# Two NF4 rounds in each output-projection step, and the layer norm's chain at its end, in a decoder layer on one core

## The chip, the core and the metric

The kernel runs on one core of a Trainium2 chip. The metric is the device time of one execution in microseconds (us). Engines: PE is the matrix engine, DVE, ACT and POOL the vector, scalar and GpSimd engines, SP the engine that here only issues DMAs; ACT and POOL issue some as well.

## The reference

One post-norm decoder layer in float32, for a batch of 4 sequences of 512 positions, width 512, 16 heads of 32:

```
x = layernorm(x + self_attention(x, wq, wk, wv, wo))        # 8 kv heads, rotary embedding, causal
x = layernorm(x + cross_attention(x, ctx, Wq, Wkv, Wout))   # causal mask over the first 512 of 1601 keys
x = layernorm(x + ffn(x, nf4(w1), nf4(w2), nf4(w3)))        # silu(x w1') * (x w2'), then w3'; inner width 1408
```

The three FFN weights pass through an NF4 round trip inside the kernel: blocks of 64 are scaled by their largest magnitude, each value goes to the nearest of 16 levels, and it is multiplied by a scaler that was itself quantised to 8 bits.

## The kernel before, in words

**Steps.** Eight blocks b = 0..7 (0 to 3 are self attention of the four sequences, 4 to 7 cross attention) of eight steps p = 0..7; a step (b, p) handles two heads. PE's program is one list written out by hand (from L1100 on): scores of the heads (`scores`, L935, turned: keys on partitions), row maxima two steps ahead (`maxima`, L902), weighting of the values (`weigh`, L959), the products of the next block's q, k, v (`make`, L886 to L888), and in step (b, 1) the output projection of block b - 1 (`project_out(b-1, k)`, k = 0, 1; same lines; 24 products each). Each fp32 product is three products of high and low parts.

**Banks.** All units that PE writes for one use (four score units `exp`, `rows`, `raw`, `out`, `round`) share two PSUM banks in the order of `ring_order()`: unit i waits until unit i - 2 has been read. A `round` is freed by DVE's `scale_rounded` (L1651), an `exp` by ACT's exponential (L1327), an `out` by DVE's two additions of `add_residual` (L1521, L1522). The maxima have one PSUM tile of their own: in self attention DVE's reduction (L1497) of one unit must end before PE's next; in cross attention (L1492) the two heads are waited for one by one.

**NF4 rounds.** 48 rounds, 20 during self attention and 28 during cross. One round takes a chunk of the divided weights: SP loads it (`load_round`: `x4`, L478, then the stores of the round before, L488, then the scalers `dqb`, L482), four comparison passes 0 to 3 run on ACT (`exceed`, L1304) or DVE (L1637), PE sums them (`rounding`, L1061, 16 products), DVE multiplies (L1651). Pass 3 overwrites the loaded chunk and waits for the other three; there is one such buffer, so the load of round u waits for PE's round u - 1. `round_of(b, p)` gives each step at most one round: (1,1) to (3,4), and (4,1) to (7,4). `scalar_passes` gives ACT pass 0, in self attention's steps 3 and 4 passes 0, 1, 3, in its step 5 passes 0, 3. ACT runs pass 0 ahead of the last exponential of the step.

**Stacks.** The heads' q and k go by six SP DMAs (`load_stacks`, L453 to L465) into four slots; SP loads those of step (b, p) + 3 after the round's load in its list. They wait for the last score unit of the step before, which frees the slot, and in self attention for POOL, which rotates and splits q and k (L668 to L685). In self attention only step 5 of a block makes nothing for the next block on PE; POOL rotates there.

**Layer norm** of block b - 1 in steps 1 to 3 of block b, on DVE: step 1 `add_residual` 0, maxima, `moments` 0 (L1528), `add_residual` 1; step 2 `moments` 1 after the first maxima, `spread` (mean, variance and a Newton inverse root on 128x4 values: L1814 to L1834, a chain of 16 tiny dependent instructions and more) after pass 3, ahead of the last maxima and of `scale_rounded`; step 3 `scale_rows` (L1538, four of 128x512). SP stores the result in step 4. POOL's `weighed` (L697 to L701) is started in every even step by DVE's `over_sums` (L1515), which stands just ahead of pass 3.

**FFN.** After block 7, `FTILES` tiles g; PE makes two hidden products (L1171), and from g = 2 on `ffn_contribute(g-1)` (L1201). At g = 1 PE does the last two output projections; the first contribution waits for both `out` units to be read. DVE at g = 1: `add_residual` 0, `moments` 0, `layer_norm` of two rows' tiles, and only then `add_residual` 1; the other half of the norm at g = 2.

Of the kernel before, what the change touches and what calls it, by code (L numbers as in the profile page):

```python
# [30 lines left out]
NP = NH // 2  # L31
# [67 lines left out]
FIRST_ROUND = NP + 1  # L99
CROSS_HOME = B * NP + 1  # L100


def round_of(b, p):

    at = b * NP + p
    u = at - FIRST_ROUND if at < FIRST_ROUND + SELF_ROUNDS else at - CROSS_HOME + SELF_ROUNDS if at >= CROSS_HOME else -1
    return u if 0 <= u < ROUNDS else None
# [8 lines left out]
def scalar_passes(u):  # L116

    b, p = divmod(u + FIRST_ROUND, NP)
    return {3: (0, 1, 3), 4: (0, 1, 3), 5: (0, 3)}.get(p, (0,)) if u < SELF_ROUNDS and b < B - 1 else (0,)
# [23 lines left out]
def ring_order():  # L143
# [3 lines left out]
    for b in range(NB):  # L147
        for p in range(NP):
# [5 lines left out]
            order += [("exp", b, p, 2), ("exp", b, p, 3)]  # L154
            order += [("raw", b + 1, what) for what in made(b + 1, p)]
            if p == 1 and b > 0:
                order += [("out", b - 1, k) for k in range(2)]
# [4 lines left out]
            if round_of(b, p) is not None:  # L162
                order.append(("round", round_of(b, p)))
# [3 lines left out]
def decoder_layer(nc, xs_dram, xt_dram, ctx_dram, w_self, w_cross, rope_dram, w_nat, w_t, nf_steps, nf_limits,  # L167
# [56 lines left out]
    with ctx:  # L224
# [207 lines left out]
        def _(sp):  # L432
# [88 lines left out]
            for b in range(NB):  # L521
                for p in range(NP):
# [6 lines left out]
                    if round_of(b, p) is not None:  # L529
# [8 lines left out]
                    if (b, p) == (1, 0):  # L538
# [10 lines left out]
                    if (b, p) == (NB - 1, 5):  # L549
                        store_round(ROUNDS - 1)  # L550
# [325 lines left out]
        def _(pe):  # L876
# [222 lines left out]
            for b in range(NB):  # L1099
                for p in range(NP):  # L1100
# [25 lines left out]
                    if p == 1 and b > 0:  # L1126
                        project_out(b - 1, 1)
                    if fore and (whats or p == 1):
# [3 lines left out]
                    if round_of(b, p) is not None:  # L1132
                        rounding(round_of(b, p))
# [87 lines left out]
        def _(act):  # L1221
# [134 lines left out]
            for b in range(NB):  # L1356
                for p in range(NP):
                    turn1, u = after(b, p, 1), round_of(b, p)
                    mine = scalar_passes(u) if u is not None else ()
# [14 lines left out]
                    if 0 in mine:  # L1374
# [551 lines left out]
```

## Time and profile before

| | us |
|---|---|
| median of 3 runs | 1232.68 (1232.57 to 1236.12) |
| profiled execution: its own time | 1232.01 |
| its span, first to last instruction | 1230.1 |
| PE busy | 1065.7 (87%) |
| DVE busy | 776.0 (63%) |
| ACT, POOL busy | 471.8, 464.5 (38% each) |
| mean granted PE clock | 0.939 |

The span is what the trace's clock counts; the execution's own time is 1.9 us longer. Of the chain of work that ended last, PE is 60%, DVE 18%, ACT 6%, DMA 6%. PE's clock is granted at 2.4 GHz (1.0) or 1.2 GHz (0.5). Steps 0 to 7 of block 1 run from 165.7 to 288.4 us, block 2 to 413.2, block 3 to 534.4, the cross blocks to 639.9, 755.2, 860.4 and 946.8, and the FFN from there to the end.

### The profile page before, as it was taken

The page shows a single profiled execution, that of the slowest core. Times are in us where ns is not written, and L with a number is a line of the kernel's source. Part 1 is how long each engine was busy: PE and PEld are TensorE (multiplying, and loading weights), DVE is VectorE, ACT ScalarE, POOL GpSimd, SP SyncE. Part 2 cuts the span into 40 slices and gives each one's busy share as a digit, 9 for nine tenths or more (in the row PEclk, how much of TensorE's full clock was granted, in tenths as well). Part 3 has the DMA queues.
Part 4 walks back from the last instruction along what each step waited for, and adds up shares of the span by engine and source line. Part 5 has one row for each costly group of instructions (what it writes and reads, how often), then busy time and mean ns, then how long its engine had stood idle before and what let it go on. Part 6 is the DMA issues. An engine that isn't in the chain of part 4 may idle for free.

```text
span 1230.1 us, 17427 instructions
## 1 busy us (share of the span) xinstructions
PE 1065.7 (87%) x6248; PEld 689.7 (56%) x6248; DVE 776.0 (63%) x1564; ACT 471.8 (38%) x580; POOL 464.5 (38%) x500
## 2 busy tenths in 40 slices
PE   6888888987988887888989778889878899999995
PEld 4545445543554353455556445555634788888884
DVE  6786657666676567547775775677494745455444
ACT  3342352645354543552553464446445021202110
POOL 4537874785378534232242232223435500000000
PEclk9798899999998898998899888989989999999998
DMA  6731563476356734733664483447556210302010
GB/s 205 213 68 43 140 165 107 133 203 179 102 152 159 201 108 118 168 68 93 148 177 95 104 208 87 105 130 175 146 126 180 83 51 1 103 1 69 1 69 34
DMA packets 81809, 145.13 MB, mean 118 GB/s; under 512 B 14984, under 2 KB 31728, under 8 KB 81468
## 3 DMA queue, kind: packets, MB, share of 16 engines
q1 hardware_dynamic: 68812, 104.03, 32.3%
q0 software_dynamic: 11888, 39.73, 11.2%
q8 instruction: 50, 0.82, 0.3%
q10 hardware_dynamic: 1024, 0.26, 0.1%
q14 instruction: 35, 0.29, 0.1%
HBM read 78.09 MB, written 23.73 MB: 83 GB/s over the span
## 4 chain that ended last, share of the span: by engine, by line
PE 60%; DVE 18%; ACT 6%; DMA 6%; issue 5%; POOL 3%; SPq 2%; ACTq 1%; DVEq 0%; POOLq 0%
PE att_pv L959 10%; PE att_scores_T L886 7%; PE att_scores_T L1201 7%; PE att_scores L1171 6%; PE att_pv L1171 6%; PE att_scores_T L887 6%; PE att_scores_T L888 6%; PE att_scores L902 6%; PE att_scores_T L935 3%; ACT att_probs L1327 3%; DMA att_k_stack<-att_k_lo 2%; DVE att_scores L1492 2%; DMA att_nf_home<-nf_dequantised_rows 2%; PE att_scores_T L1061 2%; DVE att_mx L1497 2%
## 5 line engine op out<-in xcount | busy, mean ns | idle before, releaser
L1327 ACT ACTIVATE att_probs<-att_scores_T 128x1024 f32<-128x1024 f32 (+2 forms) x256 | 219.6, 884 | 296.6 <-PE att_scores_T L935 293.9
L959 PE MATMUL att_pv<-att_probs,att_v 128*32 128x512 f32 (+3 forms) x1024 | 221.4, 557 | 1.3 <-POOL att_probs L741 0.9
L959 PE MATMUL att_pv<-att_probs,att_ones 128*32 128x512 f32 (+3 forms) x1024 | 221.4, 557 | 0.0
L1497 DVE TENSOR_REDUCE att_mx<-att_scores 128x2 f32<-128x1024 f32 x124 | 151.7, 1223 | 102.7 <-PE att_scores L902 101.6
L902 PE MATMUL att_scores<-att_k_stack,att_q_stack 96*128 96x256 f32 (+1 forms) x504 | 170.1, 415 | 43.8 <-DVE att_mx L1497 20.8
L935 PE MATMUL att_scores_T<-att_q_stack,att_k_stack 97*128 97x512 f32 (+2 forms) x512 | 147.1, 399 | 31.7 <-DVE att_nf_zone L1651 26.2
L1492 DVE CUSTOM_DVE_ANT_0 att_scores<-att_scores,att_cmask 128x128 f32<-128x128 f32 (+3 forms) x256 | 120.9, 512 | 72.0 <-PE att_scores L902 71.7
L741 POOL TENSOR_SCALAR_AFFINE_SELECT att_probs<-att_probs 128x256 f32<-128x256 f32 x128 | 59.0, 461 | 251.4 <-ACT att_probs L1327 249.0
L902 PEld LDWEIGHTS att_scores<-att_k_stack,att_q_stack 96*128 96x128 f32 x504 | 91.5, 203 | 88.9 <-DVE att_mx L1497 28.2
L935 PEld LDWEIGHTS att_scores_T<-att_q_stack,att_k_stack 97*128 97x128 f32 x512 | 90.9, 202 | 75.6 <-DVE att_nf_zone L1651 39.8
L959 PEld LDWEIGHTS att_pv<-att_probs,att_v 128*32 128x32 f32 x1024 | 51.3, 115 | 112.1 <-issue 91.3
L697 POOL TENSOR_TENSOR att_pv_raw<-att_pv_raw,att_sums_turned 128x512 f32<-128x512 f32 x32 | 45.5, 1423 | 166.7 <-DVE att_sums_turned L1515 166.7
L1407 ACT ACTIVATE att_probs<-att_scores 128x512 f32<-128x512 f32 x44 | 26.3, 598 | 213.7 <-PE att_scores L1171 213.7
L1742 DVE TENSOR_TENSOR att_probs<-att_probs,att_pv 128x512 f32<-128x512 f32 x44 | 30.2, 687 | 114.3 <-PE att_pv L1171 114.3
L886 PE MATMUL att_scores_T<-att_x_hi,att_w_hi 128*128 128x512 f32 x160 | 70.4, 440 | 21.8 <-ACT att_probs L1327 11.7
L887 PE MATMUL att_scores_T<-att_x_lo,att_w_hi 128*128 128x512 f32 x160 | 67.7, 423 | 0.0
L888 PE MATMUL att_scores_T<-att_x_hi,att_w_lo 128*128 128x512 f32 x160 | 67.2, 420 | 0.0
L886 PE MATMUL att_scores_T<-att_w_hi,att_o_hi 128*128 128x512 f32 x128 | 51.8, 404 | 5.7 <-ACT att_probs L1327 5.7
L1521 DVE TENSOR_TENSOR att_y<-att_scores_T,att_y 128x512 f32<-128x512 f32 x16 | 11.1, 691 | 69.9 <-PE att_scores_T L888 69.9
L886 PEld LDWEIGHTS att_scores_T<-att_x_hi,att_w_hi 128*128 128x128 f32 x160 | 33.2, 207 | 35.0 <-ACT att_probs L1327 18.3
L888 PE MATMUL att_scores_T<-att_w_hi,att_o_lo 128*128 128x512 f32 x128 | 51.2, 400 | 0.0
L887 PE MATMUL att_scores_T<-att_w_lo,att_o_hi 128*128 128x512 f32 x128 | 51.1, 400 | 0.0
(251 smaller groups left out, 2181.6 us busy)
## 6 DMA issues: line engine op xcount, KB each, us to landing
att_q_stack<-att_q_hi SPq DMA_DIRECT2D x128, 128.0 KB, 3.1
att_probs<-nf_x SPq DMA_DIRECT2D x28, 352.0 KB, 3.6
att_nf_home<-nf_reciprocals POOLq DMA_DIRECT2D x48, 176.0 KB, 4.2
att_q_stack<-att_q_lo SPq DMA_DIRECT2D x64, 128.0 KB, 3.6
att_k_stack<-att_k_hi SPq DMA_DIRECT2D x64, 128.0 KB, 3.4
att_nf_home<-nf_x SPq DMA_DIRECT2D x20, 352.0 KB, 3.5
w_nf<-att_nf_zone SPq DMA_DIRECT2D x192, 22.0 KB, 2.6
att_k_stack<-att_k_hi SPq DMA_DIRECT2D x64, 64.0 KB, 2.7
```

The source lines that it names most:

```text
L741: pool.affine_select(out=v, in_=v, compare_op=ALU.is_ge, fill=0.0, base=0, pattern=[[0, 2], [1, P]], channel_multiplier=-1).then_inc(kept, 1)
L886: T.matmul(out, a_hi, b_hi, start=start, stop=False)
L887: T.matmul(out, a_hi, b_lo, start=False, stop=False)
L888: return T.matmul(out, a_lo, b_hi, start=False, stop=stop)
L902: last = T.matmul(sco[:, r, 0:width], qst[0:96, s, r, P * t:P * t + P], kst[0:96, r if crossed(b) else 0, s, 0:width], start=True, stop=True)
L935: last = T.matmul(bank[:, at:at + S - q0], kst[0:97, r if crossed(b) else 0, s, P * t:P * t + P], qst[0:97, s, r, q0:S], start=True, stop= ...
L959: last = T.matmul(pv[HD * j:HD * j + HD, sums, q0:S], lhs, pr[:, at:at + S - q0], start=(t == 0), stop=(t == TT - 1))
L1171: last = T.matmul(bank, ffn_weight(w, f, kt), x[:, kt, :], start=kt == 0 and i == 0, stop=kt == KT - 1 and i == 1)
L1201: last = T.matmul(fpy[:, t, :], h[:, g % 2, P * t:P * t + P], ffn_rows(f), start=f == 0 and i == 0, stop=f == FT - 1 and i == 1)
L1327: A.activation(probs_of(b, r)[:, 1024 * h:1024 * h + w], bank[:, 0:w], ACT.Exp, scale=SCALE).then_inc(st_free, 1)
L1492: V.tensor_tensor_reduce(out=sco[:, r, 0:width], in0=sco[:, r, 0:width], in1=cmask[:, S - width:S], scale=1.0, scalar=NEG, op0=ALU.add, op ...
L1497: V.tensor_reduce(mx[:, p % 2, :].rearrange("p (r t) -> p r t", r=2)[:, :, t], sco[:, :, :], AX.X, ALU.max).then_inc(sc_free, 1)
```

## The change

1. Rounds. `round_of` becomes a list `ROUND_STEPS`. Step (b, 1) has two rounds, `mid` and `end`, for b = 1 to 6; self attention's step 5 has none, and (3, 4) has none any more; the last round, the 48th, is the `mid` of (7, 1), where it was in (7, 4). ACT's passes 0, 1, 3 stay in (1,3), (1,4), (2,3), (2,4).
2. Step (b, 1) of PE is: `project_out` 0, maxima 2, round `mid`, `project_out` 1, then `make` (x0, for a cross block to come), maxima 3, `weigh`, round `end`. Before, `make`'s first half stood ahead of the projection, and there was no `mid`.
3. Step (b, 1) of DVE ends with `scale_rounded(end)`, `moments` 1, `spread`, and the cut of x0. `scale_rows` moves to step 2, two tiles after the first maxima and two after the second. SP stores in step 3.
4. SP's list: the stacks come ahead of the round's load, except the stacks of a new block's first step (`fresh`, issued in step 5), which stay behind it.
5. FFN: both `add_residual` and both `moments` at g = 1; `layer_norm` of each half at g = 2 and g = 3.

```diff
+def round_steps():
+    steps = []
+    for b in range(1, NB):
+        for p in range(NP):
+            if b < B and p == 5 or b == B - 1 and p > 3 or (b, p) in ((1, 0), (B, 0)):
+                continue
+            steps += [(b, p)] * (2 if p == 1 else 1)
+    return steps[:ROUNDS]
+def rounds_of(b, p):
+    us = [u for u, step in enumerate(ROUND_STEPS) if step == (b, p)]
+    return tuple((us if p == 1 else [None] + us) + [None, None])[:2]
 def scalar_passes(u):
-    return {3: (0, 1, 3), 4: (0, 1, 3), 5: (0, 3)}.get(p, (0,)) if u < SELF_ROUNDS and b < B - 1 else (0,)
+    return (0, 1, 3) if b < B - 1 and p in (3, 4) else (0,)
...
 # SP
-                    if round_of(b, p) is not None:
-                        load_round(round_of(b, p))
-                    if nxt and pairs(*nxt) >= SLOTS:
+                    fresh = nxt and nxt[0] > b and nxt[1] == 0
+                    if nxt and pairs(*nxt) >= SLOTS and not fresh:
                         load_stacks(*nxt)
...
+                    for u in rounds_of(b, p):
+                        if u is not None:
+                            load_round(u)
+                    if fresh:
+                        load_stacks(*nxt)
...
-                    if p == 4 and b > 0:
+                    if p == 3 and b > 0:
                         store(b - 1)
 # PE
-                    make(b + 1, whats, 0)
                     if p == 1 and b > 0:
                         project_out(b - 1, 0)
-                    if fore and not (crossed(b) and p == 0):
                         maxima(*fore, 2)
-                    make(b + 1, whats, 1)
-                    if p == 1 and b > 0:
+                        if mid is not None:
+                            rounding(mid)
                         project_out(b - 1, 1)
+                        for half in range(2):
+                            make(b + 1, whats, half)
...
 # DVE
+                    if p == 1 and b > 0:
+                        maxima(*fore, 0)
+                        maxima(*fore, 1)
+                        exceeds(mid, range(4))
+                        add_residual(b - 1, 0)
+                        maxima(*fore, 2)
+                        if mid is not None:
+                            scale_rounded(mid)
+                        moments(b - 1, 0)
+                        exceeds(end, (1, 2))
+                        add_residual(b - 1, 1)
+                        exceeds(end, (3,))
+                        maxima(*fore, 3)
+                        if end is not None:
+                            scale_rounded(end)
+                        moments(b - 1, 1)
+                        spread(range(TT))
+                        for what in made(b + 1, p):
+                            cut_raw(b + 1, what)
+                        continue
                     if p == 2 and b > 0:
-                        moments(b - 1, 1)
-                    if p == 3 and b > 0:
                         scale_rows(range(0, 2), TT - 1)
...
                 if g == 1:
-                    add_residual(NB - 1, 0)
-                    moments(NB - 1, 0)
-                    layer_norm(range(2))
-                    add_residual(NB - 1, 1)
-                    moments(NB - 1, 1)
-                if g == 2:
-                    layer_norm(range(2, TT))
+                    for k in range(2):
+                        add_residual(NB - 1, k)
+                    for k in range(2):
+                        moments(NB - 1, k)
+                if g in (2, 3):
+                    layer_norm(range(2 * (g - 2), 2 * (g - 2) + 2))
```

## Rows read from the trace of the kernel before

**Rows 1.** View of waits, whole run: engine, line, released by; total us, times, longest.
```profile
PE att_scores_T L935 <- DVE att_nf_zone L1651: 26.2, 11, 5.6
PE att_scores_T L1061 <- ACT att_nf_home L1304: 6.9, 2, 3.5
PE att_scores_T L1201 <- DVE att_y L1522: 3.9, 1, 3.9
```
**Rows 2.** View of waits, 635 to 870 us.
```profile
PE att_scores L902 <- DMA att_k_stack<-att_k_lo: 8.0, 4, 3.5
```
**Rows 3.** View of waits, 911 to 935 us: steps (7,3) and (7,4).
```profile
PE att_scores_T L1061 <- DVE att_probs L1637: 4.5, 2, 2.7
```
**Rows 4.** Timeline of PE, (1,1) to (1,3): start, us, what, [idle before].
```profile
187.15 0.40 PE L886 MATMUL att_scores_T<-att_w_hi,att_o_hi 128*128 128x512 f32 x1
192.73 0.63 PE L902 MATMUL att_scores<-att_k_stack,att_q_stack 96*128 96x512 f32 x2
195.03 0.63 PE L1061 MATMUL att_scores_T<-att_nf_zone,att_nf_steps 128*32 128x352 bf16 x12
215.38 1.13 PE L935 MATMUL att_scores_T<-att_q_stack,att_k_stack 97*128 97x512 f32 x2 [3.66 <-DVE att_nf_zone L1651]
```
**Rows 5.** Timeline of DVE, step (1,2): first of `spread`, and the maximum behind it.
```profile
207.68 0.06 DVE L1814 MEMSET att_newton<- 128x4 f32 x1
213.67 1.23 DVE L1497 TENSOR_REDUCE att_mx<-att_scores 128x2 f32<-128x1024 f32 x1
```
**Rows 6.** Timeline of POOL, step (4,2), during `spread`.
```profile
574.57 1.51 POOL L697 TENSOR_TENSOR att_pv_raw<-att_pv_raw,att_sums_turned 128x512 f32<-128x512 f32 x1 [1.44 <-DVE att_sums_turned L1515]
```
**Rows 7.** Timeline of DVE in the FFN: the norm's second half, POOL idle.
```profile
979.53 0.06 DVE L1814 MEMSET att_newton<- 128x2 f32 x1
982.16 1.00 DVE L1538 TENSOR_SCALAR att_y<-att_y,att_mean_var,att_newton 128x512 f32<-128x512 f32 x2
```
**Rows 8.** Timeline of DVE, (4,3): cut of an x half; two tiles scaled.
```profile
581.28 1.22 DVE L1443 TENSOR_TENSOR att_x_lo<-att_raw,att_x_hi 128x1024 fp32r<-128x1024 f32 x1
583.25 1.09 DVE L1538 TENSOR_SCALAR att_y<-att_y,att_mean_var,att_newton 128x512 f32<-128x512 f32 x2
```
**Rows 9.** Timeline of PE, steps (4,1) to (4,3).
```profile
565.97 0.34 PE L1061 MATMUL att_scores_T<-att_probs,att_nf_steps 128*32 128x352 bf16 x4
568.79 0.48 PE L902 MATMUL att_scores<-att_k_stack,att_q_stack 96*128 96x256 f32 x2
581.42 0.80 PE L935 MATMUL att_scores_T<-att_q_stack,att_k_stack 97*128 97x512 f32 x1 [2.54 <-DVE att_nf_zone L1651]
```
**Rows 10.** View of groups of instructions, shapes apart: busy us, mean ns, idle before.
```profile
L1528 DVE BATCH_NORM_STATS2 att_stats<-att_y 128x6 f32<-128x512 f32 x32 | 20.5, 681 | 0.2
```
**Rows 11.** Stretches: us; busy PE, PEld, DVE, ACT, POOL; clock; DMA share; GB/s.
```profile
382.80:389.60 6.80, 5.86 (x28) 3.08 (x32) 2.87 (x4) 2.78 (x3) 6.42 (x5) 0.50 0.31 81
580.70:590.90 10.20, 9.05 (x38) 6.63 (x39) 6.21 (x18) 3.62 (x5) 1.43 (x3) 0.50 0.64 153
642.20:645.60 3.40, 3.40 (x24) 2.42 (x17) 1.97 (x10) 1.17 (x2) 0.35 (x1) 0.50 0.86 248
263.30:341.80 78.50, 67.13 (x449) 39.15 (x445) 52.43 (x80) 33.35 (x37) 43.00 (x46) 1.00 0.56 152
```
**Rows 12.** Timeline of SP and PE around the start of step (6,0).
```profile
753.52 0.61 SPq L461 DMA_DIRECT2D att_k_stack<-att_k_lo  x1
757.23 0.51 PE L902 MATMUL att_scores<-att_k_stack,att_q_stack 96*128 96x256 f32 x2 [1.63 <-DMA att_k_stack<-att_k_lo]
```
**Rows 13.** Timeline of SP and PE in step (1,5).
```profile
254.80 0.60 SPq L465 DMA_DIRECT2D att_k_stack<-att_k_lo  x1
258.50 0.63 PE L1061 MATMUL att_scores_T<-att_nf_zone,att_nf_steps 128*32 128x352 bf16 x12 [3.46 <-ACT att_nf_home L1304]
```
**Rows 14.** Tile att_nf_home: a pass on ACT; its DMAs to landing.
```profile
L1304 ACT ACTIVATE att_nf_zone<-att_nf_home,att_nf_limits x24: 1449/1458/1464, 181.8 to 492.5; 128x1408 bf16<-128x1408 bf16 x24
DMA to landing us min/median/max: 1.9/3.6/8.6
```

More of the change, by code:

```diff
@@ L154, in ring_order @@
             order += [("exp", b, p, 2), ("exp", b, p, 3)]
+            mid, end = rounds_of(b, p)
+            if p == 1 and b > 0:
+                order.append(("out", b - 1, 0))
+                if mid is not None:
+                    order.append(("round", mid))
+                order.append(("out", b - 1, 1))
             order += [("raw", b + 1, what) for what in made(b + 1, p)]
-            if p == 1 and b > 0:
-                order += [("out", b - 1, k) for k in range(2)]
             if (b, p) == (0, 2):
@@ L161, in ring_order @@
                 order.append(("dq",))
-            if round_of(b, p) is not None:
-                order.append(("round", round_of(b, p)))
+            if end is not None:
+                order.append(("round", end))
     return order + [("out", NB - 1, k) for k in range(2)]
@@ L1131, in _ @@
                     weigh(b, p, 1)
-                    if round_of(b, p) is not None:
-                        rounding(round_of(b, p))
+                    if end is not None:
+                        rounding(end)
                     if (b, p) == (0, 2):
@@ L1357, in _ @@
                 for p in range(NP):
-                    turn1, u = after(b, p, 1), round_of(b, p)
-                    mine = scalar_passes(u) if u is not None else ()
+                    turn1, (mid, end) = after(b, p, 1), rounds_of(b, p)
+                    mine = scalar_passes(end) if end is not None else ()
                     exponential(b, p, 0)
@@ L1373, in _ @@
                         hi_of_x(*halved(b, p))
-                    if 0 in mine:
-                        exceed(u, 0)
+                    if mid is not None:
+                        for k in scalar_passes(mid):
+                            exceed(mid, k)
+                    elif 0 in mine:
+                        exceed(end, 0)
                     exponential(b, p, 3)
-                    for k in mine[1:]:
-                        exceed(u, k)
+                    for k in mine if mid is not None else mine[1:]:
+                        exceed(end, k)
                     if (b, p) == (B - 1, 0):
@@ L1686, in _ @@
                         largest_behind(b, p, 1)
+                    if p == 2 and b > 0:
+                        scale_rows(range(2, TT), TT - 1)
                     if p % 2 == 0 and pairs(b, p) > 0:
                         sums_of(G)
[L1689 to L1690 removed]
                     if (b, p) == (0, 2):
@@ L1698, in _ @@
                         order_dequantised()
-                    exceeds(u, (1, 2))
-                    if closing:
-                        add_residual(b - 1, 0)
+                    exceeds(end, (1, 2))
                     if fore:
@@ L1704, in _ @@
                         largest_behind(b, p, 2)
-                    if closing:
-                        moments(b - 1, 0)
-                        add_residual(b - 1, 1)
                     if p % 2 == 0 and pairs(b, p) > 0:
@@ L1711, in _ @@
                         reciprocals()
-                    exceeds(u, (3,))
-                    if p == 2 and b > 0:
-                        spread(range(TT))
+                    exceeds(end, (3,))
                     if crossed(b + 1):
@@ L1721, in _ @@
                         largest_behind(b, p, 3)
-                    if u is not None:
-                        scale_rounded(u)
+                    if end is not None:
+                        scale_rounded(end)
                     if fore and not early:
```

27 lines of the change are left out of this document (13 added, 14 removed).

## Prediction

> **What bounds the kernel now.** I read the page first, then the view of waits, then the timelines around its longest waits, then the stretches at low clock. The page has PE busy 87% of the span and 60% of the ending chain, DVE 18%: the kernel is PE's list of work plus the places where PE stands still. The waits say where. 26.2 us in 11 waits are PE's second score unit waiting for DVE's last act of a round; 6.9 us are rounds waiting for a pass on ACT; 3.9 us is the FFN's first contribution waiting for `add_residual` [rows 1]. Four waits for stacks make 8.0 us in the cross blocks [rows 2], and two rounds waiting for DVE's passes 4.5 us in (7,3) and (7,4) [rows 3]. The reader is to see that nearly all of them concern the rounds. The clock is the second half of the story: after a wait PE often runs at 1.2 GHz for a stretch, 3.4 to 10.2 us long, in which it is busy nearly all the time [rows 11]; a matmul-bound stretch at half clock costs about half its length.
>
> **Part 1, the norm's chain.** The 3.66 us ahead of 215.38 is one of the seven entries to a step (b, 3) behind the 26.2 us [rows 4]: `spread` stands ahead of the last maxima and the round's multiplication and takes 213.67 - 207.68 = 6.0 us [rows 5]. It is slow because of its company. In the FFN the same instructions take 982.16 - 979.53 = 2.6 us with POOL idle [rows 7]; in step 2 POOL's `weighed` starts just ahead of `spread` and runs through it [rows 6]. At the end of step 1 POOL has nothing large, except in block 3 and in (7,1), so I take 2.7 there, with 6.0 as the other bound.
> The Trainium skill, page "SBUF — State Buffer", section "Who interferes with whom", says that a DVE instruction with two SBUF inputs and a GpSimd instruction that reads SBUF lock each other out for a whole instruction. Rows 5 to 7 agree (6.0 against 2.6 us). By that rule the new place is not free either in the cross steps, where POOL's causal selections read SBUF; it changes no term below.
>
> What is late next: behind the round's end DVE now does the multiplication (half a microsecond), `moments` 2 x 0.68 [rows 10], `spread` 2.7, in blocks 3 to 7 the cut 1.22 [rows 8], and then the first maximum, 1.23 in self attention [rows 5] (0.45 for one head in cross): 5.8 us in self, 6.3 in cross. PE reaches the second maxima of the step after two score units, a maxima and a weighting, about 3.8 us in self, and 568.79 - 566.31 = 2.5 in cross [rows 9]. So a new wait of 2.0 us stands in each self step 2, and of 3.8 in each cross one.
> - Blocks 1 and 2: the 3.66 becomes 2.0 plus 0.4 (below), and step 2's DVE work then ends before PE's; gain about 0.8 each: 1.6.
> - Blocks 4 to 6 are bound by DVE from the round's end to step 3: 581.42 - 566.31 = 15.1 us [rows 9]. The change takes 2.0 off `spread` and puts 2 x 1.09 of scaling in [rows 8]. No gain; POOL still runs its short causal selections there, for which I allow 0.5 each: -1.5.
> - Block 3: POOL's load of the next x waits for x0's transposition, which now comes after the projection, and its 2.4 us subtractions queue behind it into `spread`. I count -1.6.
> - Block 7: no round in (7,2), so the bank wait at (7,3) goes, about 4, and POOL's conversions for the FFN slow `spread` by about 2: +2.
> The sum is +0.5. Bounds: if every chain is 6.0, 7 x 3.3 = 23 worse; if none of the new waits showed, 20 better.
>
> **Part 2, two rounds in step 1.** The number of rounds is the same, so PE's 0.7 us each only moves. New is that the second projection needs the first's bank two units on: both additions, 2 x 0.69, against a maxima and a round; 0.4 us of wait, 7 times: -2.8. Does the second round wait for its data? Its load is issued when PE has done the first. It lands 3.6 us later [rows 14], ACT's pass is 1.46: ready at +5.4. PE has 192.73 - 187.15 = 5.6 us of projection [rows 4], and 195.03 - 192.73 = 2.3 of maxima and weighting, with the 0.4: it comes at +8.3. Covered up to a landing of about 6.3, as DVE's last pass takes the rest; at the longest, 8.6 [rows 14], it would wait 2.3 us. I take nothing. Lower bound nothing, upper 7 x 2.3 = 16. SP's list in the step is two loads and four stores longer than before, and both fit in its 21 us.
>
> **Part 3, no round in self attention's step 5.** The 6.9 us in two waits go, but the stacks of the next block are next: the last k load is issued at 254.80 behind POOL's split, and PE, ready for the round at 258.50 - 3.46 = 255.0 and two score units further, would be there at about 256.2 [rows 13]. With landings of 1.9 to 3.6 [rows 14] the load is in at 256.7 to 258.4: 0.5 to 2.2 us stays in each. I take 1.0: gain 6.9 - 2.0 = 4.9.
>
> **Part 4, rounds done by (7, 1).** The 4.5 us [rows 3] go whole: +4.5. Nothing else I see is late there, as DVE and ACT only lose work.
>
> **Part 5, stacks first.** At (6,0) PE waits 1.63 us for a load issued at 753.52, at the end of SP's list of the step, behind the round's load, four stores and scalers, some 3 us of issuing [rows 12]. Its source and its slot were ready long before. The same stands at (5,0) and (7,0); the three are 8.0 - 3.5 = 4.5 us [rows 2], and a lead of 3 us covers each: +4.5. The fourth, 3.5 us at (5,6), is a `fresh` one and stays. What is moved back is the round's load, by up to 1.7 us in (b, 6), where SP has no air; ACT's pass there is ahead of an exponential with about 2 us of air. I take nothing; bound -1.7 in each of ten short steps.
>
> **Part 6, FFN.** `add_residual` 1 no longer queues behind half a norm: 3.9 us go [rows 1]. The two halves of the norm, 2.6 + 1.0 each [rows 7], go at g = 2 and 3 behind DVE's part of the tile, and PE needs DVE again only after a tile's eight or sixteen products; uncovered they would cost up to 3.6. I take them as covered: +3.9.
>
> **The clock.** After the stack wait at (5,0) PE ran 3.4 us at half clock [rows 11], so 1.7 lost; the same after (6,0), (7,0), one of the waits of part 4 and that of part 6. Those five waits vanish: 5 x 1.7 = 8.5. Where a wait only shrinks, the low clock may stay: block 2's step 5 has 6.8 us of it [rows 11], block 1's 3.4, the entries of (1,3) and (2,3) 3.4 each: 17 us of stretch, 8.5 of loss, of which I take half, 4.2, since 263.30 to 341.80 stayed at full clock through waits of 2.0 us [rows 11]. In the cross blocks (580.70, 10.2 us) I take no change: the wait moves from the entry of step 3 into step 2.
>
> **The sum.** 0.5 - 2.8 + 4.9 + 4.5 + 4.5 + 3.9 = 15.5 of waits, and 8.5 + 4.2 = 12.7 of clock: 28.2 us. Against the profiled execution's own 1232.0 (span 1230.1, 1.9 outside it), 1203.8. It lies within 0.7 of the median, 1232.68. I forecast **1205**, a microsecond held back for the x loads that now share SP's and POOL's issue with two rounds.
>
> **The rivals.**
> - A, the norm's chain in step 1 costs PE more than the bank wait did (slower). If `spread` stays at 6.0 us there, each of seven chains ends 3.3 later, and as the maxima have one PSUM tile, PE stands 5.3 (self) to 7 us (cross) each time: 23 us. Such waits bring the low clock, 1.7 to 5 us a time as in rows 11; with 1.7, 12 more: 1205 + 35 = 1240. It decides on the other side from a chain of about 5.5 us with the clock lost. For it: no `spread` inside the blocks is near 2.6, as rows 5 shows for one. Against: rows 7. 8%.
> - B, the waits go and the clock does not come back: 1205 + 12.7 = 1218. For it: low stretches also start where I see no long wait. 17%.
> - C, the second round comes too late, by 2.3 us and its clock: 7 x 2.3 = 16: 1221. For it: landings up to 8.6. 6%.
> - D, stacks first only moves the wait: the round's load, now behind six issues in steps of 8 to 10 us, holds ACT's pass and with it an exponential. The 4.5 + 5.1 of part 5 are lost: 1215. 7%.
> - E, the cross blocks' 10.2 us stretches move to where PE waits for DVE anyway: half of some 17 us back: 1196. 15%.
> - F, no change to be measured: everything removed is found again one step on. 5%, 1232.
>
> **Numbers.** My own forecast has 42%, with a range of 1197 to 1213. The range that should hold 8 in 10 goes from E's 1192 to past C's, 1224. A measurement of this kernel tells about 0.3% (3.7 us) from no change. Faster: my own and B to E, 87%; same 6%; slower 7%.
>
> **What would show it.** `spread` in 2.6 to 3.3 us at the end of (1,1), (4,1); a wait of 2 and of 3 to 4 us at the second maxima of (b, 2), for L1497 and L1492; none for L1651 at the score units of (1,3), (2,3), (7,3); the stack waits at (5,0), (6,0), (7,0) gone; no wait for L1304 in (1,5), (2,5), a wait of 1 us for k stacks behind them; the first contribution of the FFN right behind its hidden products; a mean granted clock near 0.955. The forecast is wrong if `spread` is over 5 us in its new place, if PE waits for L1637 or L1304 at the second round of step 1, or if the clock stays at 0.939.

## The result, and the profile after

The changed kernel takes 1226.08 us (median of 6 runs, 1223.02 to 1228.35), the kernel before 1233.73 beside it (6 runs); the ratio is 0.9934, with a 95% interval of 0.9911 to 0.9956: 8 us faster, where 27 were forecast. 1226 lies outside the range of 1192 to 1224.

From the profile's page after (span, busy time by engine, clock in 40 slices):
```profile
span 1221.1 us, 17427 instructions
PE 1056.3 (87%) x6248; PEld 679.9 (56%) x6248; DVE 761.5 (62%) x1566; ACT 471.2 (39%) x578; POOL 466.1 (38%) x500
PEclk9789989999999887999899899989989999999998
```
PE's busy time fell from 1065.7 to 1056.3 us. The rest of the span, in which PE stands, was 1230.1 - 1065.7 = 164.4 and is 1221.1 - 1056.3 = 164.8. So none of the forecast 15.5 us of waits is gained, and in this profile the clock gave 9.4 of its 12.7.

View of waits, PE, whole run (engine, line, released by; total us, times, longest):
```profile
PE att_scores L921 <- DVE att_mx L1525: 34.2, 30, 8.1
PE att_scores L921 <- DVE att_mx L1520: 30.3, 31, 3.9
PE att_scores_T L1080 <- DVE att_nf_home L1665: 18.7, 5, 11.3
PE att_scores_T L1087 <- DVE att_nf_zone L1652: 5.9, 1, 5.9
PE att_pv L978 <- POOL att_probs L760: 5.0, 3, 2.0
PE att_scores L921 <- DMA att_k_stack<-att_k_lo: 3.9, 3, 2.9
```
What [rows 1] shows is gone: no score unit waits for a round's bank, no round for a pass on ACT, and the FFN's first contribution waits for nothing. In its place the maxima (L1525 and L1520; L1497 and L1492 before, with 32.2 us) hold PE for 64.5 us, and one round waits 11.3 us.

I summed for each step (from its first exponential on ACT to that of the next step) its length less PE's busy time, in two profiles of either kernel (the two below are in the experiments), and took means:

| where PE stands, us | before | after | gained | forecast |
|---|---|---|---|---|
| steps (b, 1) to (b, 3), all b | 55.2 | 51.7 | 3.5 | -0.4 (parts 1, 2; 1.9 of 4) |
| (1, 4) to (1, 6) and (2, 4) to (2, 6) | 10.8 | 7.5 | 3.3 | 4.9 (part 3) |
| (2, 7) | 0.5 | 11.2 | -10.7 | 0 |
| (7, 4) to (7, 7) | 4.9 | 4.5 | 0.4 | 2.7 (part 4) |
| (5, 0), (6, 0), (7, 0) | 7.2 | 3.4 | 3.8 | 4.5 (part 5) |
| (4, 6), (5, 6), (6, 6) | 5.8 | 8.2 | -2.4 | 0 |
| FFN | 19.9 | 16.0 | 3.9 | 3.9 (part 6) |
| (0, 7) | 1.7 and 6.6 | 6.6 and 7.8 | -3.1 | 0 |
| the rest | 56.8 | 55.5 | 1.3 | 0 |

The places of (2, 7) and (3, 2) are the two long ones. Chain of waits after, 396 to 425 us (start us, us, what), the part that ends in (2, 7):
```profile
394.74 2.57 POOL att_q_lo L689
...
397.32 0.40 SPq L574
...
398.28 0.47 SPq L575
...
402.85 13.39 DMA att_nf_home<-nf_x
...
416.26 1.12 DVE att_nf_zone L1665 x2
```
And the timeline of ACT and of PE there:
```profile
416.26 1.47 ACT L1329 ACTIVATE att_nf_zone<-att_nf_home,att_nf_limits 128x1408 bf16<-128x1408 bf16 x1 [10.66 <-DMA att_nf_home<-nf_x]
...
419.15 1.07 PE L1080 MATMUL att_scores_T<-att_nf_zone,att_nf_steps 128*32 128x352 bf16 x12 [11.26 <-DVE att_nf_home L1665]
```
The round's load of (2, 7), 352 KB, takes 13.4 us. Ahead of it stand 1.5 MB of cross weights in three loads (L574 twice, L575; the last issued at 398.28) and six loads of stacks; the last of the three weights' loads took 11.5 us itself and landed at 409.8. In the profile of before the same load took 3.4 us.

### The profile page after: what moved, and what is told of

It reads as the page before. It is cut to its first block, busy times and chain, and to the rows that moved or that the text cites. A ratio compares the mean times of both kernels' runs of the same rounds, so it can differ in the third digit from the quotient of the medians.

```text
span 1221.1 us, 17427 instructions
## 1 busy us (share of the span) xinstructions
PE 1056.3 (87%) x6248; PEld 679.9 (56%) x6248; DVE 761.5 (62%) x1566; ACT 471.2 (39%) x578; POOL 466.1 (38%) x500
## 3 DMA queue, kind: packets, MB, share of 16 engines
q0 software_dynamic: 11888, 39.73, 11.3%
## 4 chain that ended last, share of the span: by engine, by line
PE 44%; DVE 12%; DMA 3%; issue 3%; POOL 2%; ACT 2%; SPq 2%; ACTq 1%; DVEq 0%; POOLq 0%
PE att_pv L978 7%; PE att_scores L1196 7%; PE att_pv L1196 7%; PE att_scores_T L1226 6%; PE att_scores L921 4%; PE att_scores_T L905 3%; PE att_scores_T L907 3%; PE att_scores_T L906 3%; DVE att_scores L1520 2%; DMA att_probs<-nf_x 2%; PE att_scores_T L954 2%; PE att_scores_T L1080 2%; ACT att_probs L1352 1%; DMA att_nf_home<-nf_x 1%; DVE att_nf_zone L1665 1%
## 5 line engine op out<-in xcount | busy, mean ns | idle before, releaser
L921 PE MATMUL att_scores<-att_k_stack,att_q_stack 96*128 96x256 f32 (+1 forms) x504 | 173.0, 418 | 68.6 <-DVE att_mx L1525 34.2
L1525 DVE TENSOR_REDUCE att_mx<-att_scores 128x2 f32<-128x1024 f32 x124 | 151.8, 1224 | 100.5 <-PE att_scores L921 100.0
L1520 DVE CUSTOM_DVE_ANT_0 att_scores<-att_scores,att_cmask 128x128 f32<-128x128 f32 (+3 forms) x256 | 120.9, 511 | 46.3 <-PE att_scores L921 46.3
L954 PE MATMUL att_scores_T<-att_q_stack,att_k_stack 97*128 97x512 f32 (+2 forms) x512 | 143.5, 393 | 3.7 <-ACT att_v L1257 2.1
L905 PE MATMUL att_scores_T<-att_x_hi,att_w_hi 128*128 128x512 f32 x160 | 65.9, 412 | 23.7 <-ACT att_probs L1352 13.6
L907 PE MATMUL att_scores_T<-att_x_hi,att_w_lo 128*128 128x512 f32 x160 | 63.8, 399 | 0.0
L906 PE MATMUL att_scores_T<-att_x_lo,att_w_hi 128*128 128x512 f32 x160 | 63.8, 399 | 0.0
L1329 ACT ACTIVATE att_nf_zone<-att_probs,att_nf_limits 128x1408 bf16<-128x1408 bf16 x28 | 41.1, 1466 | 47.1 <-DMA att_probs<-nf_x 47.1
L1329 ACT ACTIVATE att_nf_zone<-att_nf_home,att_nf_limits 128x1408 bf16<-128x1408 bf16 x24 | 35.1, 1461 | 46.0 <-DMA att_nf_home<-nf_x 46.0
L1080 PE MATMUL att_scores_T<-att_nf_zone,att_nf_steps 128*32 128x352 bf16 x576 | 33.2, 337 | 21.1 <-DVE att_nf_home L1665 18.7
```

The lines of the kernel that those rows point to most:

```text
L905: T.matmul(out, a_hi, b_hi, start=start, stop=False)
L906: T.matmul(out, a_hi, b_lo, start=False, stop=False)
L907: return T.matmul(out, a_lo, b_hi, start=False, stop=stop)
L921: last = T.matmul(sco[:, r, 0:width], qst[0:96, s, r, P * t:P * t + P], kst[0:96, r if crossed(b) else 0, s, 0:width], start=True, stop=True)
L954: last = T.matmul(bank[:, at:at + S - q0], kst[0:97, r if crossed(b) else 0, s, P * t:P * t + P], qst[0:97, s, r, q0:S], start=True, stop= ...
L1329: A.activation((over + [x4])[k], x4, ACT.Sign, bias=limits[:, 4 + k:5 + k]).then_inc(over_act, 1)
```

## Experiments

All are edits of the changed kernel, unless they say before. Ratios are to the kernel before, run beside them on the same chip.

### Who is to blame for (2, 7): the order of loads, the bytes, or the shorter step

**The order of loads undone.**
```
-                    if nxt and pairs(*nxt) >= SLOTS and not fresh:
-                        load_stacks(*nxt)
 ...
                     for u in rounds_of(b, p):
                         if u is not None:
                             load_round(u)
+                    if nxt and pairs(*nxt) >= SLOTS:
+                        load_stacks(*nxt)
```


> The changed kernel with one part undone: in SP's list the rounds' loads stand ahead of the stacks again. Theory (my rival D, with a place I had not seen): in (2, 7) the round's load waited 13.4 us for its landing because 1.5 MB of cross weights and the stacks, now ahead of it, were under way; with the order of before it lands within 6 us, PE's wait of 11.3 us at that round shrinks to under 4 and the low clock behind it goes (some 4 us more). In exchange the three stack waits at (5, 0), (6, 0), (7, 0) are back, 1.2 to 1.6 us each, with their low clock. Sum: 1226 - 7 - 4 + 4.5 + 5 = about 1224. Rival theory (the order has no part in the wait of (2, 7), the weights alone fill the queue): the 11 us stay and the stack waits come on top, 1235.

Measured: 1222.78 us (12 runs), ratio 0.9928 [0.9895, 0.9961]. The timeline of SP and of PE:
```profile
404.23 0.47 SPq L572 DMA_DIRECT2D att_rope_tab<-w_cross  x1
...
405.57 0.58 SPq L493 DMA_DIRECT2D att_nf_home<-nf_x  x1
...
420.93 0.48 PE L1077 MATMUL att_scores_T<-att_nf_zone,att_nf_steps 128*32 128x352 bf16 x4 [7.14 <-DVE att_nf_home L1662]
```
Neither theory's number: the wait shrinks to 7.1 us, not under 4. With the order of before the load stands right behind the weights, 1.3 us after their last issue, and still lands after 11.2 us. So the order is at most a part of the cause: 4.1 us of the 11.3, by these two profiles. (5, 0), (6, 0) and (7, 0) stand 6.3 us again instead of 3.4, and (4, 6) to (6, 6) 4.7 instead of 8.2: in the cross blocks the two orders are worth the same here.

**The bytes moved away.**
```
-                    if (b, p) == (B - 2, 6):
+                    if (b, p) == (B - 2, 7):
                         sp.wait_ge(lo_ok, len(TURNED))
                         ... the cross weights' loads
```


> The changed kernel with the cross weights' two loads and the table's (1.5 MB) issued one step later, behind the stacks and the round's load of (2, 7) instead of ahead of them. Theory: these bytes are the convoy that the round's load stands in. Then its load lands within 5 us of issue, PE's 11.3 us at the round of (2, 7) fall under 1, and the 10.2 us at half clock behind go: 1226 - 10.5 - 5 = 1210. Rival: POOL's load of the residual (1 MB) and the pieces fill the engines anyway: the load still needs 8 us or more, PE waits 6 or more, time 1220 to 1226. Second rival: the weights come late for ACT in (3, 0) and PE waits there for their conversion: over 1226.

Measured: 1214.28 us (6 runs), ratio 0.9877 [0.9839, 0.9915]. SP's timeline:
```profile
401.96 0.58 SPq L493 DMA_DIRECT2D att_nf_home<-nf_x  x1
...
405.08 0.43 SPq L574 DMA_DIRECT2D att_swapped<-w_cross  x1
```
PE's waits from 386 to 425 us:
```profile
PE att_scores_T L1080 <- DVE att_nf_home L1665: 2.2, 1, 2.2
```
The load lands after 4.3 us, and the 11.3 us are gone; the 2.2 that the view shows are those of (3, 0), 2.0 in the changed kernel. The weights' bytes are what the round's load was held by, and not POOL's load of the residual (1 MB), which stayed where it was. PE stands 153.5 us in this profile, 11.3 less than in the changed kernel's; its busy time, though, is 1059.0, 2.7 more, so the low clock that I expected back is not there in sum. By the timed runs the edit is worth 0.9934 - 0.9877, 7 us, where 16 were expected.

**The step made long again.**
```
-            if b < B and p == 5 or b == B - 1 and p > 3 or ...
+            if b == 1 and p == 5 or b == B - 1 and p > 2 or ...
```


> The changed kernel with a round back in (2, 5) and none in (3, 3), so that the self blocks still do twenty. It tells apart what makes PE wait at the round of (2, 7). Theory now (part 3 is the cause, not the order of loads): the cross weights' 1.5 MB are issued when POOL has split the last key and query rows, some 22 us after the start of (2, 5) by POOL's own work; the step is 5.7 us shorter without its round, so that the next round's load comes 0.9 to 4.1 us behind the weights' last issue instead of 7.2, lands after 11 to 14 us instead of 3 to 4, and PE waits. With the round back in (2, 5) the distance is over 7 us, the load lands within 5 and PE's wait at (2, 7) is under 2; (2, 5) waits 3.5 for its round and takes 14.4 us. Time 1226 - 11 - 5 + 3.4 + 2 = about 1215. Rival (stacks first is the cause, as in my rival D): (2, 7) still waits 7 us or more, 1226 or above.

Measured: 1220.99 us (6 runs), ratio 0.9926 [0.9900, 0.9953]. SP's timeline:
```profile
399.59 0.47 SPq L575 DMA_DIRECT2D att_rope_tab<-w_cross  x1
...
408.75 0.58 SPq L493 DMA_DIRECT2D att_nf_home<-nf_x  x1
```
PE's waits from 377 to 420 us:
```profile
PE att_scores_T L1080 <- DVE att_nf_home L1665: 4.5, 1, 4.5
```
The stretch of (2, 7) (columns as in [rows 11]):
```profile
409.40:419.00 9.60, 9.06 (x66) 4.21 (x67) 6.04 (x8) 5.50 (x6) 3.98 (x6) 1.00 0.82 211
```
With stacks still first and the weights where they were, (2, 7) has no wait left: 9.60 - 9.06 = 0.5 us. The 4.5 us are the round in (2, 5) itself, a microsecond more than before's 3.47 there. For the wait my theory holds: stacks first by itself doesn't make it. For the time it missed: 1221 where 1215 was expected, halfway to the rival's 1226, and the ratio can't be told from the change's (0.9926 and 0.9934), so that the wait's going is shown by the trace and not by the timed runs. In the profile PE stands 8.5 us less than in the changed kernel's first, but is busy 5.7 us longer (1061.9 against 1056.3). Why the shorter step does it: SP issues the weights when POOL has finished the last low part (the 2.57 us from 394.74 in the chain above). POOL's row of rotations and splits does not get shorter, but step (2, 5) does, by 14.4 - 8.7 = 5.7 us, so PE's round of (2, 6), which the next round's load waits for, moves up to the weights. Time from the weights' last issue to the round's load, and the load's landing, in all profiles that load the weights in this place:

| kernel | behind the weights, us | landing, us |
|---|---|---|
| before (two profiles) | 7.7, 7.6 | 3.4, 3.5 |
| before with the FFN's change | 7.7 | 3.4 |
| round back in (2, 5) | 9.2 | 4.2 |
| before with stacks first | 7.6 | 5.2 |
| norm later | 5.5 | 8.3 |
| changed kernel (two profiles) | 4.6, 4.6 | 13.4, 12.5 |
| POOL's subtractions early | 4.6 | 13.9 |
| order undone | 1.3 | 11.2 |

The step's length and the order work together. In (2, 7) PE stands 0.5 us in the kernel before, 0.5 with stacks first alone, 7.6 with the short step alone (the changed kernel, order undone) and 11.2 with both (mean of two profiles). So 7 us are the short step's, and some 3.6 the stack loads' that the order puts between the weights and the round's load.

The Trainium skill, page "DMA: Bandwidth & Descriptors", section "Queues, rings and completion order", says that each transfer engine consumes the descriptors of one queue in ring order. The trace agrees: issued 1.3 to 5.5 us behind the weights on SP's queue, the load lands after 8 to 14 us, and in no profile ahead of the weights; in the changed kernel it is 6.4 us behind the last of them.

### The norm's chain

**POOL's subtractions ahead of their wait.**
```
+                    if (b, p) == (B - 1, 1):
+                        ... lo_of_weights(h, ...)
                     if crossed(b + 1) and p in (1, 2):
                         ... wait for x0, load_x(*nxt)
 ...
-                    if (b, p) == (B - 1, 1):
-                        ... lo_of_weights(h, ...)
```
First what the changed kernel shows in (3, 1), timelines of DVE and of POOL:
```profile
461.63 5.17 DVE L1861 TENSOR_SCALAR att_newton<-att_mean_var 128x4 f32<-128x4 f32 x1
466.84 0.17 DVE L1863 TENSOR_SCALAR att_newton_int<-att_newton 128x4 int32<-128x4 int32 x1
...
462.12 2.36 POOL L724 TENSOR_TENSOR att_w_lo<-att_swapped,att_w_hi 128x1024 fp32r<-128x1024 f32 x1
464.43 2.34 POOL L724 TENSOR_TENSOR att_w_lo<-att_turned,att_w_hi 128x1024 fp32r<-128x1024 f32 x1
```


> The changed kernel with POOL's two subtractions of the cross weights' low parts (2.35 us each) put ahead of its wait for x0 in (3, 1), so that they run some 20 us earlier. Theory: in (3, 1) the norm's chain was held 5.2 us in one 4-element instruction that ended when POOL's second subtraction ended; without them the chain takes 2.3 us as in (1, 1), PE's wait at the second maxima of (3, 2) falls from 8.1 to 3.5, and of the 17.1 us at half clock some 7 go: 1226 - 4.6 - 3.4 = 1218. Rival: the long instruction waited for something else (the cuts, the statistics): the wait stays over 7 us, 1226. What could spoil it: the subtractions now hold a maxima or a pass of the round in (3, 0) or (3, 1) for up to 4.7 us.

Measured: 1220.72 us (12 runs), ratio 0.9911 [0.9882, 0.9940]. DVE's and PE's timeline:
```profile
469.22 0.17 DVE L1861 TENSOR_SCALAR att_newton<-att_mean_var 128x4 f32<-128x4 f32 x1
...
474.02 0.50 PE L921 MATMUL att_scores<-att_k_stack,att_q_stack 96*128 96x512 f32 x1 [3.13 <-DVE att_mx L1525]
```
An instruction on four elements a partition takes 0.17 us, or 5.17 when POOL works beside it. It had begun before POOL's two, while POOL issued loads, and ended 0.03 us behind the second. In the five profiles in which the two subtractions follow it, it took 5.17 to 5.20 us. The wait fell from 8.1 to 3.1 as expected, and steps (3, 0) to (3, 2) take 56.3 us instead of 62.8 and 61.4 in the changed kernel's two profiles; the ratio fell by 0.2%, within the intervals, so the gain is shown by the trace and not by the timed runs. What I had named as a spoiler is there too: in (3, 0) a pass of the round on DVE now takes 4.9 us instead of 0.6, for half a microsecond of PE's time. The rule that the prediction took from the Trainium skill (page "SBUF — State Buffer", section "Who interferes with whom") also lists `tensor_scalar` among what can take the pair of ports that GpSimd uses, and the trace agrees; I had read only its half on two inputs.

**The norm's chain behind the second maxima of (b, 2).**
```
                         moments(b - 1, 1)
-                        spread(range(TT))
 ...
                         maxima(*fore, 1)
+                    if p == 2 and b > 0:
+                        spread(range(TT))
```


> The changed kernel with the norm's chain behind the second maxima of (b, 2) instead of at the end of (b, 1), still ahead of POOL's products; the four scalings follow in one go. Theory of part 1 (the chain is 2.2 us of DVE work in DVE's list and PE waits for the list, not for the chain's place): in the cross blocks PE's wait at the second maxima falls from 3.7 to about 1.5 us, but comes back at the third or fourth maxima or the entry of step 3, as DVE has as much to do between the round and there: no change, within 5 us of 1226. In block 3 the chain is then clear of POOL's two subtractions: 8.1 falls to 3 or less, 5 to 8 us with the clock: 1219. Rival: DVE has air later in (b, 2): 3 x 2.2 + 5 and half of some 30 us at half clock come back, 1205 to 1212.

Measured: 1214.94 us (6 runs), ratio 0.9863 [0.9833, 0.9893]. PE's waits in (4, 2), 567 to 590 us:
```profile
PE att_scores L921 <- DVE att_mx L1520: 4.5, 3, 3.3
```
And in (2, 6) and (2, 7), 382 to 420 us:
```profile
PE att_scores L921 <- DMA att_k_stack<-att_k_lo: 3.9, 1, 3.9
PE att_scores_T L1080 <- DVE att_nf_home L1665: 3.0, 1, 3.0
```
In the cross steps the wait only moves from the second to the third maxima (3.71 us to 3.34): DVE is the bound there, wherever the chain stands, as theory had it. The ratio gained 7 thousandths, more than I expected. Of the 11.4 us that PE stands less in this profile, the largest single part is not the chain's: a stack 3.9 us late in (2, 6) put the round's load 5.5 us behind the weights, and (2, 6) and (2, 7) together stand 7.9 instead of 12.9 us. Block 3 gave 2.1 of its own. What made the stack late I did not follow up.

### Stacks first, alone

The kernel before, with the rounds' load moved behind the stacks as in the change and nothing else.

> The kernel before with one part of the change alone: stacks ahead of the round's load in SP's list (but for the first stack of the next block). Theory: the waits at (5, 0), (6, 0), (7, 0) go, 4.5 us, and three stretches of 3.4 us at half clock, 5.1: 1233.7 - 9.6 = 1224, unless the round's load is late somewhere else. From the changed kernel I expect it late in (2, 7), as the cross weights are in the queue there: PE waits 4 to 10 us more, so that 1226 to 1234 comes out. Rival: no such wait without the double rounds: 1224.

Measured: 1238.24 us (12 runs), ratio 1.0060 [1.0029, 1.0091]: slower by itself. The timeline of SP and of ACT in (4, 6):
```profile
625.27 0.58 SPq L478 DMA_DIRECT2D att_probs<-nf_x  x1
...
632.84 1.47 ACT L1307 ACTIVATE att_nf_zone<-att_probs,att_nf_limits 128x1408 bf16<-128x1408 bf16 x1 [5.92 <-DMA att_probs<-nf_x]
```
The three stack waits went (7.2 to 3.4 us of standing), but the round's load, behind six loads of stacks, is issued 1.9 us into (4, 6) instead of 0.6 ahead of it, and takes 7.5 us to land instead of 4.0 and 3.7 in two profiles of before (7.1 and 9.6 in (5, 6) and (6, 6), instead of 5.9 to 6.6), and PE stands 11.8 us in (4, 6) to (6, 6) instead of 5.8, and 30.1 in the steps 1 to 3 of blocks 4 to 6 instead of 22.3 and 23.7. The first is my rival D, in the place where I had put it; the second, 7 us and the larger part, is in steps 1 to 3, for which I had set nothing. The wait that I expected from the weights in (2, 7) is not there: this kernel still has its round in (2, 5).

### The FFN alone

The kernel before, with the change at g = 1 to 3 alone.

> The kernel before with the change in the FFN alone: both additions first, then both statistics, the norm's halves one tile later each. Theory (part 6 of the prediction): PE's 3.9 us wait at the first contribution goes and 1.7 of clock with it: 5.6 us, 1231.5 - 5.6 = 1226, with the stretch from the last exponential to the end 5 to 6 us shorter than in the profile of before. Rival: the norm's halves in their new places hold DVE and PE waits at the second or third tile: no gain.

Measured: 1226.06 us (12 runs), ratio 0.9954 [0.9928, 0.9980]. Stretch from the last exponential to the end, this kernel's:
```profile
942.30:1220.50 278.20, 261.94 (x1184) 213.09 (x1184) 139.62 (x300) 39.41 (x58) 20.81 (x28) 0.98 0.16 52
```
And of the kernel before:
```profile
946.80:1230.10 283.30, 263.78 (x1184) 214.13 (x1184) 144.88 (x300) 39.41 (x59) 20.00 (x27) 0.97 0.15 51
```
5.1 us shorter, 3.3 of standing and 1.8 of clock. By the two ratios it makes more than half of what the whole change brings (0.9954 against 0.9934), though their intervals overlap widely.

### The same kernels again

> The kernel before, unchanged, for a second profile. Theory: PE's wait at the end of (0, 7), 0.7 us in the trace that the prediction read and 5.9 to 6.9 in the five traces since, one of them of the kernel before with stacks first alone, is a matter of luck of the one trace (transfers that land 1 to 2 us later, and DVE's casts held by POOL), not of the change: here 5 to 7 us at (0, 7). Rival: the change lengthens it: 1 us here. The stack waits at (5, 0), (6, 0), (7, 0) should be 1.2 to 1.7 us again, the other waits within 0.3 us of the first trace.

> The changed kernel, unchanged, for a second profile. Theory: the waits at (2, 7), 11.3 us, and (3, 2), 8.1 us, belong to the program and are there again within 1 us; so are 5 to 7 us at (0, 7). Rival: they are luck of one trace, then one of them is under 4 us.

Measured: before 1236.10 us, after 1218.87, one run each. PE's waits around (0, 7), 152 to 172 us, in the new profile of before:
```profile
PE att_scores_T L1068 <- DVE att_nf_zone L1624: 5.9, 1, 5.9
```
and in the one that the prediction read:
```profile
PE att_scores_T L1068 <- DVE att_nf_zone L1624: 0.7, 1, 0.7
```
The wait belongs to both kernels; one profile of before missed it. There DVE's casts are clear of POOL (0.51 us for three, 3.10 in the new profile of before, 3.21 in the changed kernel's), and PE comes to the place 2.7 us later, so that the landing, a microsecond shorter, keeps it waiting less. The long waits of the changed kernel are there again, 10.2 and 8.2 us:
```profile
PE att_scores L921 <- DVE att_mx L1525: 32.4, 29, 8.2
PE att_scores_T L1080 <- DVE att_nf_home L1665: 18.0, 5, 10.2
```

### Versions that beat both

**Three edits**: weights a step later, POOL's subtractions early, and the dequantised scalers turned in (1, 0):
```
-            if (b, p) == (0, 7):
+            if (b, p) == (1, 0):
                 order.append(("dq",))
 ... and so on PE, ACT and DVE, there in the middle of the step
```


> The changed kernel with three waits taken away at once: cross weights loaded a step later (1214.3 by itself), POOL's subtractions ahead of its wait in (3, 1) (1220.7 by itself), and PE's turning of the dequantised scalers moved from the end of (0, 7) to the middle of (1, 0), with DVE's reordering ahead of it and ACT's copy behind. At (0, 7) five traces show PE standing 5.9 to 6.9 us for scalers that land late, with 10.2 us at half clock. Theory: the three are independent: 1214.3 - 5.4 - (6 + 4) = 1199. Rival: the first round's scalers then come late and PE waits at the middle round of (1, 1) for 3 to 6 us: 1204. Second rival: the gains overlap, as the clock falls somewhere else: 1207 to 1210.

> The changed kernel with cross weights a step later, POOL's subtractions early in (3, 1), the dequantised scalers turned in (1, 0), and the norm's chain behind the second maxima of (b, 2). The first three together made 1208.4, the fourth alone 1214.9. If the fourth's gain was its own (block 3 and some of the cross blocks' low clock), 1203 to 1206; if it was the wait of (2, 7) that its shift happened to break up, and block 3, both of which the others have taken already: 1207 to 1209.

> As the kernel of four edits, but with the scalers turned at the end of (0, 7) as in the changed kernel. In the profile of three edits the turning in (1, 0) took PE's 5.9 to 7.2 us of (0, 7) away and gave 2.3 in (1, 0) and 3.0 in (1, 1) back, with 10 us of low clock for 10. Theory: worth 1 to 3 us; this kernel 1 to 3 us slower than the one of four edits. Rival: the first round comes late by it, and this kernel is the faster one, by up to 3 us.

| kernel | us | ratio |
|---|---|---|
| weights late, subtractions early, scalers in (1, 0) | 1208.43 | 0.9808 [0.9776, 0.9840] |
| the same and norm later | 1210.53 | 0.9825 [0.9792, 0.9858] |
| weights late, subtractions early, norm later | 1211.12 | 0.9849 [0.9809, 0.9889] |

The three can't be told apart: all are 1.5 to 1.9% faster than before, and 9 to 13 thousandths better than the change. The first came out at 1208.4, where 1199 was expected: the gains overlap, as the second rival of its text had it; the fourth edit's gain had been taken already, and turning the scalers elsewhere is worth less than the runs can tell. PE's waits of the first, whole run:
```profile
PE att_scores_T L1080 <- DVE att_nf_home L1665: 13.5, 5, 5.0
PE att_scores_T L1087 <- DVE att_nf_zone L1652: 2.3, 1, 2.3
```
Of the 6 us at (0, 7) 2.3 are left in (1, 0), and a 3.0 us wait for the round in (1, 1) is new; the weights, now ahead of the load for (3, 0), make that round wait 5.0 instead of 2.0 us. Moving the weights moves the place of the wait, if for less.

## Why the prediction was wrong

**The step that failed is part 3.** It said of the two self steps without their round that "the stacks of the next block are next", and named only what is late on PE's own list. The cross weights' load is not in the prediction at all, so the distance between it and the rounds' loads was silently held fixed. But its start is tied to POOL's work, and the round's load to PE's. 5.7 us taken out of (2, 5) brought the two together, and (2, 7) stands 10.7 us longer. Shown by the round put back (wait gone, bytes and order unchanged) and by the bytes moved (wait gone, step still short). Some 3.6 of the 10.7 us come only with part 5's order on top. In time it is 7 of the 19 us that are missing (0.9934 against 0.9877 with the bytes moved); the rest is below.

**Part 5** was wrong as well, and its rival D (7%) right in kind. The lead of 3 us did take the stack waits (3.8 of 4.5 us), but what "has no air", the round's load in (b, 6), cost 2.4 us in the changed kernel, and the edit alone made the kernel before 0.6% slower. I had set that loss to nothing with a bound of 1.7 a step.

**Part 1.** The chain in the new place (first and last of its rows in (1, 1)):
```profile
204.47 0.06 DVE L1852 MEMSET att_newton<- 128x4 f32 x1
...
207.04 0.16 DVE L1872 SCALAR_TENSOR_TENSOR att_newton<-att_newton 128x4 f32<-128x4 f32 x1
```
207.04 + 0.16 - 204.47 = 2.7 us, as taken from [rows 7]. The new waits came where forecast and as long:
```profile
208.52 0.50 PE L921 MATMUL att_scores<-att_k_stack,att_q_stack 96*128 96x512 f32 x1 [1.99 <-DVE att_mx L1525]
...
583.01 0.39 PE L921 MATMUL att_scores<-att_k_stack,att_q_stack 96*128 96x256 f32 x1 [3.71 <-DVE att_mx L1520]
```
2.0 and 3.8 were forecast; the four cross waits are 3.7 to 3.9 us, that of (2, 2) only 0.7. Block 3 went by the path written down, the subtractions queued behind the load of x into `spread`, at 1.1 us more of standing (11.7 against 10.6) where 1.6 was forecast; not priced was the half clock behind it. The chain there takes over 7 us, which the prediction itself had named as a sign of being wrong (over 5). **Part 2**: the second projections wait 2.4 us in seven waits for L1550, against 2.8. Steps 1 to 3 together still gained 3.5 us where I had a small loss. Most of the difference is in blocks 4 to 6, which stand as long as before (22.9 against 23.0 us) where parts 1 and 2 allowed 2.7 us more; blocks 1 to 3 did better than forecast by 2.2 us, block 7 worse by 1.2 (2.3 gained, 3.5 forecast with part 4's share). A second round late by 1.7 to 2.1 us, rival C, is there in (2, 1) alone. **Part 3's own waits**: 3.3 of 4.9 us. The stacks behind the two steps cost 0.5 us each, not 1; but in (1, 6) DVE's passes wait for the round's load, which takes 5.0 us, one of them is held by POOL (2.75 us, 0.6 without), and PE waits 2.6 us at a maxima that DVE reduces behind them. **Part 4**: the two waits went, and a new one of 2.0 us for POOL's causal selection stands in (7, 5); I had written that nothing else was late there. **Part 6** was right: 3.9 forecast and 3.9 measured, with 1.7 of clock forecast and 1.8 measured.

**The clock** was right in sum by the four profiles: busy time fell from 1065.7 and 1068.4 to 1056.3 and 1051.9, 12.9 on the mean against 12.7. With one profile of a kernel up to 4.4 us from the next, that is partly luck, and it was not right by place. Behind the two long waits the changed kernel runs (columns as in [rows 11]):
```profile
412.70:422.90 10.20, 3.75 (x22) 2.35 (x22) 4.46 (x6) 2.72 (x3) 3.83 (x5) 0.50 0.60 162
467.30:484.40 17.10, 11.38 (x50) 5.71 (x50) 12.55 (x25) 5.18 (x6) 4.83 (x5) 0.50 0.16 36
```
The second is (3, 2), with 11.4 us of work at half clock. The mean granted clock of the first profile is 0.946, from 0.939, where 0.955 was forecast. Over the six timed runs of the changed kernel its median is 0.940, and it is 0.936 to 0.941 in the three sets of runs of the kernel before: there it stayed where it was, the prediction's other sign of being wrong and what rival B had said of the clock.

**In sum** 15.5 us of waits were forecast, and none came: -10.7 at (2, 7), -2.4 in (b, 6), 1.6 less in part 3, 2.3 less in part 4, 0.7 less in part 5 and 3.1 by the chance of (0, 7), against 3.9 more in steps 1 to 3 and 1.3 in the rest. That is the table's last column against the one before it. The profiles' spans say 13 us (means of two), the timed runs 8, with an interval of 5 to 11.

## What to carry to other kernels

When a step gets shorter, list every transfer that is started by another engine's work and see what it now lands beside: loads of 1.5 MB that were harmless 7.6 us ahead of a small one cost 11 us at 4.6, with six more loads in between, and 7 us at 1.3 without them. An edit of a queue's order must be priced for what is moved back, in the step with the least air, and not only for what is moved ahead. Look for long DVE instructions on few elements: there it is not the chain that is slow, a neighbour on POOL holds it.

## What the runs showed of the hardware

- A DVE instruction held by POOL is not let in between two POOL instructions: the one of 461.63 ended behind both subtractions, 5.17 us on, though the first was over at 464.5; in four more profiles the same instruction took 5.17 to 5.20. Operations with a scalar (5.17 for 0.17), casts (3.21 for 0.51) and the round's passes (2.75 for 0.6) are held; a maximum over 128x1024 took 1.18 to 1.27 us in all of these profiles.
- Low clock and standing don't add up simply: taking the 11.3 us wait out of (2, 7) gave no busy time back (1056.3 to 1059.0). The 10.2 us at half clock there are gone in that profile, but PE had done only 3.75 us of work in them, and 6.8 us at 206.7, at full clock in the changed kernel's profile, are at half clock.
- A wait of some 6 us in (0, 7), there in eleven of the twelve profiles whose scalers are turned there and 0.7 us long in the one that the prediction read, is how much a single place can differ between profiles of one program.
